# The last chunk of a layer-norm pipeline moved to other PSUM banks, and eight small turns of a QR step done another way

## The chip, the cores and the metric

One core of one Trainium2 chip runs the whole kernel in one launch. The metric is device time in microseconds (us). The engines are named as in the profile: PE is TensorE (PEld its weight loads), DVE is VectorE, ACT is ScalarE, POOL is GpSimd, SP is SyncE, which here only issues DMAs. Each engine runs its own list of instructions in order and waits on counting semaphores. PSUM has eight banks of 2 KB per partition; PE writes them, DVE and ACT read them.

## The reference

```python
h = _L0_tok_ref(x, w, b)            # softmax over windows of 8 samples, weighted sum: 128 x 94 tokens of 64
h = h + _L0_attn_ref(_layernorm(h), ...)
h = h + _L0_ffn_ref(_layernorm(h), ...)

# inside the attention, per batch row and head:
qkv = (x @ w_qkv.T + b_qkv)
qgr, _ = jnp.linalg.qr(q)
kgr, _ = jnp.linalg.qr(k)
attn_grass = jnp.einsum('bhnd,bhmd->bhnm', qgr, kgr) ** 2 * grassman_scale
dots = jnp.einsum('bhnd,bhmd->bhnm', q, k)
a = jnp.concatenate([dots * scale, dots ** 2 * riem_scale, attn_grass], axis=1)
a = softmax(conv_w @ batchnorm(a) + conv_b);  out = a @ v
```

Q of the QR step is not formed. The kernel takes the Gram matrix of each head's 8 columns (q.T q and k.T k), eliminates it and fixes the signs, and from that makes one 8 x 8 matrix per head that stands between q and k.

## The kernel before, in words

The program is a row of blocks. At the end of a block all engines meet (a barrier), and only then does the next one begin. Four matter here.

**Constants**, up to 26.9 us. **Tokens** (`pool_project`), from there to 228.3 us: the 64 pairs of batch rows come in, are scored and softmaxed. A loop of `STEPS` = 32 steps spreads the weights over the partitions by PE into `ps_spread` (four banks), DVE and POOL multiply and sum. Behind it runs a chain for each of `NCH` = 16 chunks of four pairs (`CP`), one chunk every two steps:

- `pads(c)` on DVE completes the tokens of the chunk, `centre(c)` on PE subtracts the mean (into `ps_c`), `squares(c)` on ACT writes the squares `sq` and a copy `xc`;
- `variance(c)` on PE, `deviation(c)` on ACT and `inverse(c)` on DVE give one over the deviation;
- `rows(c, h)` on PE multiplies by the weights of q, k and v, for halves h = 0 and 1, both into the two banks of `ps_tok`; `rows_out(c, h)` on DVE scales them into `tok` and raises `drained[h]`;
- `store(c)` on SP writes `tok` to DRAM by three DMAs; `grams(c)` on PE multiplies `tok` with itself into `ps_c`, `grams_out(c)` on ACT copies that to `own`, and `gram_sum(c)` on POOL sums it into `gram`.

Since both halves of `rows` use `ps_tok`, `rows(c, 1)` waits for `rows_out(c, 0)`. Since `ps_c` holds the centred tokens and the Gram matrices alike, `centre(c)` waits for `grams_out(c - 1)`. After step 31 nothing is left of the loop but the end of chunk 14 and all of chunk 15. SP waits for all stores before it meets the others.

**QR** (`orthogonalise`), 228.3 to 287.1 us. PE turns `gram` (eight 128 x 128 pieces, into `ps_turn`), DVE copies them to `aug` after it and POOL have filled the rest of `aug`, and then works down one long list: elimination, roots, signs, back-substitution, up to `m_sum`. PE turns `m_sum` in eight pieces of 128 x 128, and DVE copies them back to `m_t` in four copies. Beside this list, ACT copies `top` (a DMA of the first eight rows of each head) into `aug`; PE turns q and k of chunks 0 to 7 (`queries_keys`, 32 turns of 96 x 64 in a chunk, each two chunks ahead of ACT's copies at most); then PE and ACT prepare ten banks of expert weights (`EXPERT_BANKS`). ACT takes the roots ahead of the copy of bank number `ROOTS_AT` = 7, counted from 0. After the banks, q and k of chunks 8 to 15 follow.

**Attention** (`attend`), the rest: PE, DVE, ACT and POOL in a loop over 64 pairs, then projection and FFN. Its first instruction of weight is POOL's `m_blk<-m_t`.

Of the kernel before, what the change touches and what calls it, by code (L numbers as in the profile page):

```python
# [287 lines left out]
def pool_project(nc, x, x_g, x_in, ps_score, tokens, gram, v_dram, qk_dram, top_dram, qk_rows, rows_in, k):  # L288
# [4 lines left out]
    with ExitStack() as ctx:  # L293
# [34 lines left out]
        def halves(view):  # L328
            return view.rearrange("p (a t) -> p a t", a=2)

        def chunk_at(i, begun):

            c, odd = divmod(i - begun, 2)
            return c if not odd and 0 <= c < NCH else None

        @block.sync
# [33 lines left out]
        def _(pe):  # L370
# [21 lines left out]
            def centre(c):  # L392
                pe.wait_ge(s["ready"], c + 1)
                if c:
                    pe.wait_ge(s["std_done"], c)
                    pe.wait_ge(s["gram_out"], c)
                pe.matmul(ps_c[:, 0:W], k["cent_w"][:], tokens[:, span(c, CP), :].rearrange("p r m -> p (r m)"),
                          start=True, stop=True).then_inc(s["cent_done"], 1)

            def variance(c):  # L400
                pe.wait_ge(s["kept"], c + 1)
                for r in range(CP):
                    mm = pe.matmul(ps_c[0:NP, W + 2 * r:W + 2 * r + 2], sq[:, r, :], k["mean_w"][:, 0:128:64], start=True, stop=True)
                mm.then_inc(s["var_done"], 1)

            def rows(c, h):
                if h:
                    pe.wait_ge(drained[0], c + 1)
                elif c:
                    pe.wait_ge(drained[1], c)  # L410
                for e in range(2):
                    for b in range(2):
                        own_rows = slice(64 * b, 64 * b + 64)
                        mm = pe.matmul(ps_tok[:, b, 192 * e:192 * e + 192], xc[own_rows, 2 * h + e, :],
                                       k["w_tok"][own_rows, b, :], start=True, stop=True)
# [15 lines left out]
            for i in range(STEPS + 4):  # L431
                if i < STEPS:
                    spread(i // HP, 2 * (i % HP))
                c = chunk_at(i, 4)
                if c is not None:
# [5 lines left out]
                if i < STEPS:  # L441
                    spread(i // HP, 2 * (i % HP) + 1)
                c = chunk_at(i, 4)
                if c is not None:
                    rows(c, 1)
                c = chunk_at(i, 3)
                if c is not None:
                    centre(c)

        def parted(eng, g, part):  # L450
# [18 lines left out]
        def _(act):  # L469
# [24 lines left out]
            def squares(c):  # L494
                act.wait_ge(s["cent_done"], c + 1)
                if c:
                    act.wait_ge(s["var_done"], c)
                    act.wait_ge(s["tok_done"], 2 * c)
                act.activation(sq[:].rearrange("p r m -> p (r m)"), ps_c[:, 0:W], ACT.Square)
                act.activation(xc[:].rearrange("p r m -> p (r m)"), ps_c[:, 0:W], ACT.Copy).then_inc(s["kept"], 1)  # L500

            def deviation(c):
                act.wait_ge(s["var_done"], c + 1)
                if c:
                    act.wait_ge(s["rstd_done"], c)
                act.activation(std[:], ps_c[0:NP, W:W + 2 * CP], ACT.Sqrt, bias=k["ln_eps"][0:NP, 0:1]).then_inc(s["std_done"], 1)

# [8 lines left out]
            for i in range(STEPS + 4):  # L516
                c = chunk_at(i, 5)
                if c is not None:
                    grams_out(c)
                c = chunk_at(i, 4)  # L520
# [4 lines left out]
                c = chunk_at(i, 3)  # L525
# [33 lines left out]
        def _(dve):  # L559
# [39 lines left out]
            def rows_out(c, h):  # L599
# [6 lines left out]
                for e in range(2):  # L606
                    for b in range(2):
                        r = 2 * h + e
                        out = dve.scalar_tensor_tensor(out=tok[:, a, r, b, :], in0=ps_tok[:, b, 192 * e:192 * e + 192],
                                                       scalar=rstd[:, a, 2 * r + b:2 * r + b + 1], in1=k["bias_row"][:, 0, :],  # L610
# [56 lines left out]
def orthogonalise(nc, p, gram, m_t, top_dram, qk_dram, qk_rows, rows_in, q_cm, k_cm, k):  # L667
# [10 lines left out]
    with ExitStack() as ctx:  # L678
# [30 lines left out]
        marks = {}  # L709

        @block.sync
        def _(sp):
# [16 lines left out]
        def _(act):  # L729
# [812 lines left out]
```

## Time and profile before

| | us |
|---|---|
| median of 3 runs | 875.92 |
| lowest, highest | 872.6, 876.63 |
| the profiled execution | 875.29 |
| its span, first to last instruction | 873.4 |
| mean granted TensorE clock, as a share | 0.941 |

The profiled execution is 1.89 us longer than its span. Times in the rows below are from the span's start.

### The profile page before, as it was taken

The page shows a single profiled execution, that of the slowest core. Times are in us where ns is not written, and L with a number is a line of the kernel's source. Part 1 is how long each engine was busy: PE and PEld are TensorE (multiplying, and loading weights), DVE is VectorE, ACT ScalarE, POOL GpSimd, SP SyncE. Part 2 cuts the span into 40 slices and gives each one's busy share as a digit, 9 for nine tenths or more (in the row PEclk, how much of TensorE's full clock was granted, in tenths as well). Part 3 has the DMA queues.
Part 4 walks back from the last instruction along what each step waited for, and adds up shares of the span by engine and source line. Part 5 has one row for each costly group of instructions (what it writes and reads, how often), then busy time and mean ns, then how long its engine had stood idle before and what let it go on. Part 6 is the DMA issues. An engine that isn't in the chain of part 4 may idle for free.

```text
span 873.4 us, 39834 instructions
## 1 busy us (share of the span) xinstructions
PE 765.1 (88%) x16837; PEld 566.1 (65%) x16837; DVE 709.7 (81%) x1376; ACT 452.7 (52%) x943; POOL 515.0 (59%) x580
## 2 busy tenths in 40 slices
PE   3478898776695799999999999999999999799994
PEld 2245454444575577777777787777777877466663
DVE  4387878775598499999999999999999999767762
ACT  2362434322344365555565566655656556477773
POOL 3244444443000688888888888888888887222220
PEclk9798879878698699999999999999999999999998
DMA  8756662662580222222222222222222221011111
GB/s 291 294 170 199 201 193 65 131 129 59 156 146 2 63 65 67 65 71 67 73 64 65 65 64 64 64 66 66 73 73 65 64 64 45 1 24 30 28 29 33
DMA packets 89198, 77.63 MB, mean 89 GB/s; under 512 B 37145, under 2 KB 79708, under 8 KB 89052
## 3 DMA queue, kind: packets, MB, share of 16 engines
q1 hardware_dynamic: 88524, 73.83, 29.4%
q8 instruction: 131, 2.15, 1.0%
q10 hardware_dynamic: 528, 1.54, 0.5%
q14 instruction: 15, 0.12, 0.0%
HBM read 59.23 MB, written 13.04 MB: 83 GB/s over the span
## 4 chain that ended last, share of the span: by engine, by line
PE 50%; DVE 11%; issue 3%; ACT 1%; POOL 0%; POOLq 0%; ACTq 0%; DVEq 0%
PE ps_dot L1091 10%; PE ps_m L1115 8%; PE ps_a L1141 7%; PE ps_a L1133 7%; PE ps_a L1227 4%; DVE row_max_o L1351 3%; DVE row_max_e L1353 3%; PE ps_a L1104 3%; DVE row_max L1339 2%; DVE sums L1371 2%; PE ps_m L1077 2%; PE ps_a L1212 2%; PE ps_dot L1184 1%; PE ps_a L1235 1%; PE ps_m L1121 1%
## 5 line engine op out<-in xcount | busy, mean ns | idle before, releaser
L1270 ACT ACTIVATE sq<-ps_dot 128x376 f32<-128x376 f32 x384 | 165.2, 482 | 152.3 <-PE ps_dot L1091 144.3
L1091 PE MATMUL ps_dot<-q_st,k_blk 64*64 64x94 f32 x6144 | 170.5, 249 | 1.1 <-ACT sq L1270 0.8
L1091 PEld LDWEIGHTS ps_dot<-q_st,k_blk 64*64 64x64 f32 x6144 | 134.6, 134 | 53.0 <-issue 28.9
L1028 POOL TENSOR_TENSOR half<-prob 128x564 f32<-128x564 f32 x64 | 75.6, 1182 | 61.3 <-ACT prob L1265 61.3
L1013 POOL TENSOR_TENSOR v_blk<-v_rep,vmask 128x384 f32<-128x384 f32 x128 | 106.8, 856 | 7.1 <-PE ps_m L1121 5.2
L549 POOL TENSOR_TENSOR x_g<-x_g,w_odd 128x752 f32<-128x752 f32 x32 | 57.0, 1780 | 89.4 <-ACT w_odd L492 89.4
L1035 POOL TENSOR_TENSOR k_blk<-k_cm,hmask 128x768 f32<-128x768 f32 x64 | 96.8, 1513 | 1.8 <-PE ps_a L1133 1.8
L1037 POOL TENSOR_TENSOR k_mix<-k_cm,cols 128x768 f32<-128x768 f32 x64 | 96.9, 1514 | 0.0
L1339 DVE TENSOR_REDUCE row_max<-ps_a 128x94 f32<-128x564 f32 x128 | 89.4, 740 | 5.9 <-PE ps_a L1141 5.7
L1141 PE MATMUL ps_a<-sq,mix_w 64*32 64x282 f32 x2048 | 82.4, 406 | 0.3 <-ACT sq L1270 0.3
L1115 PE MATMUL ps_m<-prob,v_blk 128*64 128x94 f32 x1536 | 76.6, 248 | 1.1 <-ACT prob L1265 1.1
L1262 ACT ACTIVATE prob<-prob,head_const 128x564 f32<-128x564 f32 x64 | 49.1, 767 | 51.6 <-DVE prob L1361 51.6
L1133 PE MATMUL ps_a<-q_st,k_mix 64*64 64x94 f32 x3072 | 75.4, 243 | 0.5 <-DVE prob L1361 0.3
L1064 POOL COPY w_sel<-ffn_w 128x258 f32 x64 | 25.9, 404 | 77.9 <-DVE qk_rows L1427 52.3
L1115 PEld LDWEIGHTS ps_m<-prob,v_blk 128*64 128x64 f32 x1536 | 64.8, 136 | 8.7 <-ACT prob L1265 1.7
L385 PE MATMUL ps_spread<-parts,pair_sel 128*128 128x376 bf16 x256 | 60.4, 365 | 10.0 <-POOL parts L466 10.0
L1133 PEld LDWEIGHTS ps_a<-q_st,k_mix 64*64 64x64 f32 x3072 | 68.0, 134 | 1.1 <-issue 1.0
L1346 DVE TENSOR_TENSOR k_blk<-ps_m,hmask 128x768 f32<-128x768 f32 x64 | 61.3, 957 | 7.5 <-PE ps_dot L1091 4.9
L1371 DVE TENSOR_REDUCE sums<-half 128x94 f32<-128x282 f32 x128 | 60.0, 470 | 1.7 <-POOL half L1028 1.7
L1021 POOL TENSOR_TENSOR m_blk<-m_t,mask 128x128 f32<-128x128 f32 x64 | 26.0, 407 | 57.2 <-POOLq L678 57.2
L584 DVE TENSOR_REDUCE tokens<-x_g 128x94 f32<-128x752 f32 x64 | 57.9, 924 | 0.5 <-POOL x_g L549 0.5
L1141 PEld LDWEIGHTS ps_a<-sq,mix_w 64*32 64x32 f32 x2048 | 47.6, 106 | 9.1 <-ACT sq L1270 0.7
(221 smaller groups left out, 1440.2 us busy)
## 6 DMA issues: line engine op xcount, KB each, us to landing
v_rep<-v_rows SPq DMA_DIRECT2D x128, 192.0 KB, 3.1
x_g<-in_x_dram SPq DMA_DIRECT2D x15, 1500.0 KB, 7.8
qk_rows_kept<-tok SPq DMA_DIRECT2D x16, 384.0 KB
qk_rows<-qk_rows_kept SPq DMA_DIRECT2D x4, 1536.0 KB, 11.2
v_rows<-tok SPq DMA_DIRECT2D x16, 192.0 KB
q_st<-q_cm SPq DMA_DIRECT2D x64, 47.0 KB, 1.9
out_dram<-rows SPq DMA_DIRECT2D x16, 188.0 KB
x_g<-in_x_dram ACTq DMA_DIRECT2D x1, 1500.0 KB, 7.3
```

Of the source, the lines that this page charges most:

```text
L1013: vb = pool.tensor_tensor(v_blk[:, a, b].rearrange("p t (o d) -> p (t o) d", o=H), v_rep[:, a, b].rearrange("p (t o d) -> p (t o) d", o=H, ...
L1028: pool.tensor_tensor(half[:], prob[:, a, :, 0:3, :], prob[:, a, :, 3:6, :], ALU.add).then_inc(s["half_done"], 1)
L1035: pool.tensor_tensor(k_blk[:, a, :, 0], k_cm[:, span(i, 1), :].rearrange("p i (u m) -> p (i u) m", m=4).unsqueeze(2).broadcast_to([128, NT ...
L1037: pool.tensor_tensor(k_mix[:, a].rearrange("p t x o -> p (t x) o"), k_cm[:, span(i, 1), :].rearrange("p i m -> p (i m)").unsqueeze(2).broa ...
L1091: mm = pe.matmul(ps_dot[64 * v:64 * v + 64, (2 * g + b) % 3, N * c:N * c + N], k_blk[rows, a, SLOTS * (3 * v + g) + c].rearrange("p k h m ...
L1115: pe.matmul(ps_m[64 * b:64 * b + 64, AV_AT:AV_AT + N], v_blk[:, a, b, t, :], prob[:, a, b, t, :], start=(t == 0), stop=(t == NT - 1), skip ...
L1133: mm = pe.matmul(ps_a[half_of, BANK[b][t // 3], N * (t % 3):N * (t % 3) + N], k_mix[64 * b:64 * b + 64, a, t, 8 * w:8 * w + 8].rearrange(" ...
L1141: mm = pe.matmul(ps_a[32 * c:32 * c + 32, BANK[b][v], 0:3 * N], k["mix_w"][64 * v:64 * v + 64, :], sq[64 * v:64 * v + 64, b, c].rearrange( ...
L1270: act.activation(sq[:, b, :, g, :], ps_dot[:, (2 * g + b) % 3, 0:SLOTS * N].rearrange("p (c n) -> p c n", c=SLOTS), ACT.Square).then_inc(s ...
L1339: dve.tensor_reduce(top[:, b, :], bass.AP(ps_a[:].tensor, 1024 * b, [[4 * 512, 128], [1, N], [512, 2], [N, 3]]), AX.XY, ALU.max).then_inc( ...
L1346: dve.tensor_tensor(k_blk[:, a, :, 1], ps_m[:, KT_AT:KT_AT + NP].rearrange("p (u m) -> p u m", m=4).unsqueeze(2).broadcast_to([128, NT * S ...
L1371: dve.tensor_reduce(sums[:, b], half[:, b].rearrange("p t n -> p n t"), AX.X, ALU.add).then_inc(s["sums_done"], 1)
```

## The change

It has three parts. First, the last chunk (c = `LAST` = 15) has other PSUM banks: its centred tokens and its variance go to bank 0 of `ps_spread`, and its rows of h = 0 to banks 1 and 2 of it; its rows of h = 1 stay in `ps_tok`. `centre(15)` then waits only for the tokens. PE's list has chunk 15 up to its rows in step 32, ahead of the Gram matrices of chunk 14, and these of chunk 15 wait for `grams_out(14)`. ACT's list has `squares(15)` and `deviation(15)` in step 32 too, ahead of `grams_out(14)`. Second, the eight turns of `gram` are `transpose` where they were `matmul` with the identity. Third, of the four copies of turned sums into `m_t`, ACT takes the two of partitions 64 to 127.

```diff
+        def centred(c):
+            return ps_spread[:, 0, :] if c == LAST else ps_c[:]
+
+        def rows_bank(c, h, b):
+            return ps_spread[0:NP, 1 + b, :] if c == LAST and h == 0 else ps_tok[:, b, :]
...
             def centre(c):
                 pe.wait_ge(s["ready"], c + 1)
-                if c:
+                if 0 < c < LAST:
                     pe.wait_ge(s["std_done"], c)
                     pe.wait_ge(s["gram_out"], c)
...
             def rows(c, h):
-                if h:
+                if h and c < LAST:
                     pe.wait_ge(drained[0], c + 1)
-                elif c:
+                elif c and (h or c < LAST):
                     pe.wait_ge(drained[1], c)
...
                 pe.wait_ge(s["std_done"], c + 1)
+                if c == LAST:
+                    pe.wait_ge(s["gram_out"], c)
...
+                if i == STEPS:
+                    centre(LAST)
+                    variance(LAST)
+                    for h in range(2):
+                        rows(LAST, h)
...
+                if i == STEPS:
+                    squares(LAST)
+                    deviation(LAST)
...
+        def turned_back(b, n):
+
+            q = slice(64 * b, 64 * b + 64)
+            return (m_t[q, :, 4 * n:4 * n + 4].rearrange("p i d -> p d i"),
+                    ps_turn[q, 2 + n, :].rearrange("p (d i b) -> p d i b", d=4, b=2)[:, :, :, b])
...
+            for n in range(2):
+                act.wait_ge(m_turned, n + 1)
+                act.activation(*turned_back(1, n), ACT.Copy)
...
-                for b in range(2):
-                    q = slice(64 * b, 64 * b + 64)
-                    step(dve.tensor_copy(m_t[q, :, 4 * n:4 * n + 4].rearrange("p i d -> p d i"),
-                                         ps_turn[q, 2 + n, :].rearrange("p (d i b) -> p d i b", d=4, b=2)[:, :, :, b]))
+                step(dve.tensor_copy(*turned_back(0, n)))
...
-                mm = pe.matmul(ps_turn[:, e // 4, 128 * (e % 4):128 * (e % 4) + 128], gram[:, :, e], k["ident"][:], start=True, stop=True)
+                mm = pe.transpose(ps_turn[:, e // 4, 128 * (e % 4):128 * (e % 4) + 128], gram[:, :, e], k["ident"][:])
```

What stands on PE at the end of the token block, before. L385 is `spread`, L397 `centre`, L403 `variance`, L414 `rows`, L426 `grams`; after the last spread come four rows of chunk 14 and four of chunk 15.

```order
L385 MATMUL ps_spread<-parts,pair_sel 128x376 x4
L397 MATMUL ps_c<-tokens,cent_w 128x384
L403 MATMUL ps_c<-mean_w,j_sq 96x2 x4
L414 MATMUL ps_tok<-w_tok,j_xc 96x192 x8
L426 MATMUL ps_c<-tok 32x32 x32
L397 MATMUL ps_c<-tokens,cent_w 128x384
L403 MATMUL ps_c<-mean_w,j_sq 96x2 x4
L414 MATMUL ps_tok<-w_tok,j_xc 96x192 x8
L426 MATMUL ps_c<-tok 32x32 x32
```

The same place of PE with the change (the lines of the five helpers are now 398, 410, 416, 427 and 441).

```order
L398 MATMUL ps_spread<-parts,pair_sel 128x376 x4
L410 MATMUL ps_c<-tokens,cent_w 128x384
L416 MATMUL ps_c<-mean_w,j_sq 96x2 x4
L427 MATMUL ps_tok<-w_tok,j_xc 96x192 x8
L410 MATMUL ps_spread<-tokens,cent_w 128x384
L416 MATMUL ps_spread<-mean_w,j_sq 96x2 x4
L427 MATMUL ps_spread<-w_tok,j_xc 96x192 x4
L427 MATMUL ps_tok<-w_tok,j_xc 96x192 x4
L441 MATMUL ps_c<-tok 32x32 x64
```

The whole chain of chunk 15 up to its rows moved ahead of the Gram matrices of chunk 14, which now stand in one row with those of chunk 15.

What stands on DVE at the end of the QR block, before (L773 is the helper of the list, L833 doubles `m_sum`, L839 copies back, L678 is the block's end).

```order
L773 TENSOR_TENSOR prods<-wq,aug 128x8
L773 TENSOR_TENSOR m_sum<-m_sum,prods 128x8
L833 COPY m_sum<-m_sum 128x8x64
L839 COPY m_t<-ps_turn 64x4x64 x4
L678 UNCONDITIONAL_BRANCH
```

And with the change.

```order
L805 TENSOR_TENSOR prods<-wq,aug 128x8
L805 TENSOR_TENSOR m_sum<-m_sum,prods 128x8
L865 COPY m_sum<-m_sum 128x8x64
L869 COPY m_t<-ps_turn 64x4x64 x2
L701 UNCONDITIONAL_BRANCH
```

Two of the four copies left DVE; they stand at the end of ACT's list, behind its last copy of k.

## Rows read from the trace of the kernel before

**Rows 1.** The head of the page: the span.

```profile
span 873.4 us, 39834 instructions
```

**Rows 2.** Timeline, chunks 14 and 15: start, duration, instruction, [idle before <-releaser].

```profile
209.68 0.16 DVE L590 TENSOR_REDUCE tokens<-tokens 128x8 f32<-128x8 f32 x1
...
211.38 1.08 PE L426 MATMUL ps_c<-tok 94*32 94x32 f32 x64 [1.64 <-issue]
...
212.52 0.38 ACT L512 ACTIVATE own<-ps_c 128x256 f32<-128x256 f32 x1 [5.78 <-PE ps_c L426]
...
213.05 1.62 PE L397 MATMUL ps_c<-tokens,cent_w 128*128 128x384 f32 x2 [0.58 <-ACT own L512]
...
217.00 1.60 PE L414 MATMUL ps_tok<-w_tok,j_xc 64*96 64x192 f32 x8
...
218.75 1.39 DVE L609 SCALAR_TENSOR_TENSOR tok<-ps_tok,j_rstd,bias_row 96x192 f32<-96x192 f32 x4 [1.14 <-PE ps_tok L414]
...
220.19 1.60 PE L414 MATMUL ps_tok<-w_tok,j_xc 64*96 64x192 f32 x8 [1.59 <-DVE tok L609]
221.93 1.39 DVE L609 SCALAR_TENSOR_TENSOR tok<-ps_tok,j_rstd,bias_row 96x192 f32<-96x192 f32 x4 [1.80 <-PE ps_tok L414]
...
224.32 0.55 SPq L351 DMA_DIRECT2D top_rows<-tok  x1
...
226.25 0.32 POOL L540 TENSOR_TENSOR gram<-own 128x64 f32<-128x64 f32 x1
```

**Rows 3.** SP's waits over the whole run: one of them.

```profile
SPq L367 <- DMA top_rows<-tok: 2.9, 1, 2.9
```

**Rows 4.** Timeline, chunk 14 at the higher clock.

```profile
203.77 0.87 PE L397 MATMUL ps_c<-tokens,cent_w 128*128 128x384 f32 x2
...
206.37 0.89 PE L414 MATMUL ps_tok<-w_tok,j_xc 64*96 64x192 f32 x8
```

**Rows 5.** Windows: stretch, length, busy time (instructions) by engine, PEclk, DMA share, GB/s.

```profile
207.00:210.40 3.40, 1.16 (x12) 0.57 (x8) 2.90 (x8) 0.00 (x0) 0.96 (x3) 0.99 0.00 0
210.50:228.20 17.70, 8.35 (x154) 5.75 (x154) 3.76 (x12) 1.90 (x5) 2.77 (x6) 0.50 0.32 71
```

**Rows 6.** Timeline, the start of the QR block.

```profile
228.33 4.16 PE L845 MATMUL ps_turn<-ident,gram 128*128 128x128 f32 x16 [3.83 <-PEq L293]
...
229.55 0.44 POOL L726 MEMSET aug<- 128x16 f32 x8 [2.98 <-DVE aug L775]
...
232.60 1.43 DVE L779 COPY aug<-ps_turn 128x512 f32<-128x512 f32 x1 [0.47 <-PE ps_turn L845]
232.99 2.04 ACT L741 ACTIVATE aug<-top 128x1024 f32<-128x1024 f32 x1 [8.05 <-DMA top<-top_rows]
...
235.76 1.09 DVE L790 TENSOR_TENSOR prods_t<-fac,aug 128x896 f32<-128x896 f32 x1
```

**Rows 7.** Timeline around the roots.

```profile
255.34 0.32 DVE L797 COPY diag<-aug 128x128 f32<-128x128 f32 x1
...
256.10 0.60 ACT L753 ACTIVATE ffn_w<-ps_turn 128x512 f32<-128x512 f32 x1 [1.16 <-PE ps_turn L877]
...
257.00 0.95 DVE L800 RECIPROCAL rs<-rs 128x128 f32<-128x128 f32 x1 [1.34 <-ACT rs L751]
```

**Rows 8.** Timeline of PE alone: q and k of chunks 2 to 7.

```profile
236.82 8.14 PE L856 MATMUL ps_turn<-ident,qk_rows 96*64 96x96 f32 x192 [0.67 <-ACT k_cm L738]
```

**Rows 9.** Timeline, the end of the QR block.

```profile
282.86 1.97 PE L885 MATMUL ps_turn<-ident,m_sum 128*128 128x128 f32 x8 [10.06 <-DVE m_sum L833]
284.08 2.56 DVE L839 COPY m_t<-ps_turn 64x256 f32<-64x256 f32 x4 [1.28 <-PE ps_turn L885]
...
287.18 0.41 POOL L1021 TENSOR_TENSOR m_blk<-m_t,mask 128x128 f32<-128x128 f32 x1 [57.19 <-POOLq L678]
```

**Rows 10.** Windows, columns as in rows 5.

```profile
232.60:234.20 1.60, 1.60 (x22) 1.60 (x24) 1.56 (x2) 1.21 (x1) 0.00 (x0) 0.50 1.00 316
...
104.60:118.20 13.60, 13.03 (x108) 7.41 (x109) 11.39 (x21) 6.25 (x11) 6.78 (x7) 0.50 0.59 194
```

More of the change, by code:

```diff
@@ L329, in halves @@
             return view.rearrange("p (a t) -> p a t", a=2)
+        LAST = NCH - 1
+        def centred(c):
+            return ps_spread[:, 0, :] if c == LAST else ps_c[:]
+        def rows_bank(c, h, b):
+            return ps_spread[0:NP, 1 + b, :] if c == LAST and h == 0 else ps_tok[:, b, :]
         def chunk_at(i, begun):
@@ L334, in chunk_at, with early_chunk_at @@
             return c if not odd and 0 <= c < NCH else None
+        def early_chunk_at(i, begun):
+            c = chunk_at(i, begun)
+            return c if c != LAST else None
         @block.sync
@@ L393, in centre @@
                 pe.wait_ge(s["ready"], c + 1)
-                if c:
+                if 0 < c < LAST:
                     pe.wait_ge(s["std_done"], c)
                     pe.wait_ge(s["gram_out"], c)
-                pe.matmul(ps_c[:, 0:W], k["cent_w"][:], tokens[:, span(c, CP), :].rearrange("p r m -> p (r m)"),
+                pe.matmul(centred(c)[:, 0:W], k["cent_w"][:], tokens[:, span(c, CP), :].rearrange("p r m -> p (r m)"),
                           start=True, stop=True).then_inc(s["cent_done"], 1)
@@ L402, in variance @@
                 for r in range(CP):
-                    mm = pe.matmul(ps_c[0:NP, W + 2 * r:W + 2 * r + 2], sq[:, r, :], k["mean_w"][:, 0:128:64], start=True, stop=True)
+                    mm = pe.matmul(centred(c)[0:NP, W + 2 * r:W + 2 * r + 2], sq[:, r, :], k["mean_w"][:, 0:128:64], start=True, stop=True)
                 mm.then_inc(s["var_done"], 1)
             def rows(c, h):
-                if h:
+                if h and c < LAST:
                     pe.wait_ge(drained[0], c + 1)
-                elif c:
+                elif c and (h or c < LAST):
                     pe.wait_ge(drained[1], c)
@@ L433, in _ @@
                     spread(i // HP, 2 * (i % HP))
-                c = chunk_at(i, 4)
+                c = early_chunk_at(i, 4)
                 if c is not None:
@@ L442, in _ @@
                     spread(i // HP, 2 * (i % HP) + 1)
-                c = chunk_at(i, 4)
+                c = early_chunk_at(i, 4)
                 if c is not None:
                     rows(c, 1)
-                c = chunk_at(i, 3)
+                c = early_chunk_at(i, 3)
                 if c is not None:
                     centre(c)
+                if i == STEPS:
[3 more added lines that the diff above has]
+                        rows(LAST, h)
         def parted(eng, g, part):
@@ L498, in squares @@
                     act.wait_ge(s["tok_done"], 2 * c)
-                act.activation(sq[:].rearrange("p r m -> p (r m)"), ps_c[:, 0:W], ACT.Square)
-                act.activation(xc[:].rearrange("p r m -> p (r m)"), ps_c[:, 0:W], ACT.Copy).then_inc(s["kept"], 1)
+                act.activation(sq[:].rearrange("p r m -> p (r m)"), centred(c)[:, 0:W], ACT.Square)
+                act.activation(xc[:].rearrange("p r m -> p (r m)"), centred(c)[:, 0:W], ACT.Copy).then_inc(s["kept"], 1)
             def deviation(c):
@@ L505, in deviation @@
                     act.wait_ge(s["rstd_done"], c)
-                act.activation(std[:], ps_c[0:NP, W:W + 2 * CP], ACT.Sqrt, bias=k["ln_eps"][0:NP, 0:1]).then_inc(s["std_done"], 1)
+                act.activation(std[:], centred(c)[0:NP, W:W + 2 * CP], ACT.Sqrt, bias=k["ln_eps"][0:NP, 0:1]).then_inc(s["std_done"], 1)
             def grams_out(c):
@@ L519, in _ @@
                     grams_out(c)
-                c = chunk_at(i, 4)
+                c = early_chunk_at(i, 4)
                 if c is not None:
@@ L524, in _ @@
                     odd_weights(i)
-                c = chunk_at(i, 3)
+                c = early_chunk_at(i, 3)
                 if c is not None:
                     squares(c)
+                if i == STEPS:
+                    squares(LAST)
+                    deviation(LAST)
                 if i < STEPS - HP:
```

4 lines of the change are left out of this document (2 added, 2 removed).

## The prediction

> **What bounds the kernel now.** The span is 873.4 us [rows 1] and the profiled execution 875.29, so 1.89 us lie outside it; the median is 875.92, 0.63 above that execution. I read the timeline first, because the three edits sit at the ends of blocks, where all engines meet and nothing of the next block can cover a delay. Three places matter.
>
> The end of the token block is one thread. The tokens of chunk 15 are complete at 209.84, but `centre(15)` starts at 213.05: it waits for ACT's `own` copy (212.52 to 212.90) of chunk 14's Gram matrices (211.38) [rows 2]. From there the thread runs centre, squares, variance, rows (217.00), `rows_out` (218.75), rows again (220.19, 1.59 us idle for DVE), `rows_out` again (221.93 to 223.32). SP issues the last of three stores at 224.32 to 224.87 and waits 2.9 us for its landing [rows 3], to about 227.8; POOL is done at 226.57. The next block's PE starts at 228.33 [rows 6]. So SP's stores end the block, POOL is 1.2 us earlier.
>
> The QR block is DVE's list, with one gate: its reciprocal at 257.00 idled 1.34 us for ACT's roots, though `diag` was ready at 255.66 [rows 7]. ACT could not take the roots sooner: they stand behind its copy of an expert bank (256.10), which had waited for PE. Going back along that queue: PE works on the experts when q and k of chunks 2 to 7 are turned, and it starts these at 236.82, after 0.67 us of idle for ACT's first copies [rows 8]; ACT is late because it waited 8.05 us for the DMA of `top`, to 232.99, and then copied 2.04 us [rows 6]. So from the block's start to the roots the time is set by this DMA, ACT and PE, and DVE has slack: about 0.9 us, if the roots (0.3 us and two hand-overs) were taken at once.
>
> The end of the block is PE's turns of `m_sum` (282.86 to 284.83), DVE's four copies (284.08 to 286.64) and the barrier; POOL starts the next block at 287.18 [rows 9].
>
> **The change, part 1: chunk 15.** `centre(15)` can start when `tokens` is ready and PE has done chunk 14's rows (209.75): at about 209.92 instead of 213.05, which is 3.13 sooner. What stands behind it on PE is the 64 Gram products of chunk 14; for them waits only ACT's `own` and POOL, costed below. Up to 210.4 the clock is at its higher level and then at the lower [rows 5]. At the lower one centre takes 1.62 and ends 1.66 before ACT starts; at the higher 0.87 [rows 2, 4]. The new one runs 0.5 us at the higher, which is 57% of it, and the other 43% cost 0.70: ACT starts 1.21 after its start instead of 1.66, 0.45 sooner. The rest up to the first `rows_out` is unchanged: 217.00 falls to 213.42, 218.75 to 215.17. The second half no longer waits for DVE: eight passes follow on PE, each 0.16 (192 columns at 1.2 GHz, and 8 x 0.16 + 0.32 is the 1.60 of the row), so they are done at 213.42 + 2.56 + 0.32 = 216.30, and DVE, busy with the first half until 216.56, goes on without a break: to about 217.93 instead of 223.32. That is 5.4 us.
>
> Does it reach the block's end? SP's path moves whole: 5.4. POOL's: chunk 14's Gram matrices now run at 216.4 to 217.5, `own` to 217.95, POOL's three sums (1.55 us) to 219.55; chunk 15's products 218.0 to 219.1, `own` must wait for those sums, 219.6 to 220.0, and POOL ends at 221.6. SP ends at 227.8 - 5.4 = 222.4, still last, with 0.8 to spare. The stores of chunk 14 have left 6 us before. The bounds of this part: if the clock is at the lower level from the start, 4.95; if it stays at the higher to the end, centre to rows takes 2.60 instead of 3.95, rows 0.89 and 0.77 more for the second half, DVE ends at 209.92 + 2.60 + 0.89 + 0.15 + 2.78 = 216.4, which is 6.9. Ahead of the fall PE was busy 1.16 of 3.40 us [rows 5]; the new centre adds about 0.5 us, still half or less, so I take 5.4.
>
> **Part 2: the turns of `gram`.** Eight matmuls in 16 passes take 4.16 us; eight transposes of that very shape, at the same clock, are 8 instructions in 1.97 [rows 6, 9]. DVE's second copy into `aug` starts at 232.60 for want of them. The first could start when POOL has filled `aug`, 229.99, so the copies would end near 232.85 instead of 234.03: 1.2 sooner. But `prods_t` reads ACT's copy of `top`, ready at 235.03, so it can start only 0.7 sooner than 235.76 [rows 6]. And all of that flows into the wait for the roots, which stand at the same distance from the block's start as before: the slack there grows from 0.9 to 1.6. This part is worth 0; the cover is the gate at 257.00, and without it the part would be worth 0.7.
>
> **Part 3: the copies back.** Four DVE copies take 2.56, so 0.64 each. With two on DVE the second starts when the last turn lands, 284.83, and ends at 285.5. ACT's pair runs beside it. The trace has no such ACT copy: one of 256 elements from PSUM took 0.38 [rows 2], the strided 1,024 of `top` 2.04 [rows 6], so 0.38 to 0.6; with the first of them a little late, ACT ends by 285.3 to 285.7. Gain 0.9 to 1.1, I take 1.0; if ACT and DVE took turns on the bank it would be 0.
>
> **The sum.** 875.29 - 5.4 - 0 - 1.0 = 868.9 for an execution like the profiled one; beside the median, 875.92 - 6.4 = **869.5**.
>
> **The rivals.**
> *A, the clock in q and k is lost.* Before, PE had no gap from 228.33 until 236.2, and the clock rose at 234.3 in it; then 192 passes took 8.14 us, 42 ns each. At the lower level 22 take 1.60, 73 ns [rows 8, 10]. Now PE has 2.2 us less to do and must still wait for ACT until 8.5 us after the block's start. At the lower clock its work ends 5.7 to 7.2 us into it, sooner if the clock rises in between: a gap of up to 3 us like the one ahead of the fall at 210.4 [rows 5]. If q and k then meet the lower clock, each microsecond costs 0.42 on the path to the roots, and nothing covers it, since ACT's queue is what DVE waits for. A low stretch of 3.5 to 7 us costs 1.5 to 2.9: 871.0 to 872.4. For it: the gap. Against: it must fall badly against the clock's own changes, about half the cases. The Trainium skill ("TensorE: Matmul & The Clock Gate", Part 4) says that the higher clock does not engage for transposes, which do not count as busy in the same way; by that rule the 2 us of transposes add to the gap and the clock rises later too. No row of this trace shows it either way: its only transposes of that size stand alone at the lower clock.
> *B, the clock holds through chunk 15.* PE's work is closer together at the fall. Part 1 gives 6.9: 868.0.
> *C, the block's end is held by something else.* If the landing of the last store or the barrier does not follow DVE whole, for instance because POOL or the two chunks' stores come into each other's way, 2 to 3 us of part 1 are lost: 871.5 to 872.5. Against: 0.8 us of room at POOL, 6 us between the stores.
> *D, slower.* The same gap as in A, but the low clock stays through q and k and into the experts: 192 x 31 ns = 5.9, and from there on every microsecond of PE's expert work at half speed costs about half of one. The gain of 6.4 is gone when the low stretch outlasts q and k by 1 us, some 15 us in all. A stretch of 13.6 us at the lower clock with PE busy 13.03 of it exists [rows 10], so it can happen; but at this place PE's passes follow without gaps, as they did at 234.3 when the clock rose. About 878 if the experts are in it.
>
> **How the numbers follow.** The forecast 0.50 (own range 868 to 871), A 0.28, B 0.11, C 0.07, D 0.04. 0.5% is 4.4 us, about what a measurement of this kernel tells from no change: faster is below 871.5, slower above 880.3. Nearly all of the forecast and B, and some 0.35 of A, are faster: 0.49 + 0.11 + 0.09 = 0.69; of D a half is slower: 0.02; the remaining 0.29 is the same. The range 867 to 873 takes in B and A.
>
> **What would show it.** DVE's last `rows_out` should end near 218 and PE's first transpose start near 223; PE should go from rows to rows of chunk 15 without idle. The eight turns should be 8 instructions in 2 us, DVE's wait for the roots longer (about 2 us), and the distance from the block's start to the reciprocal unchanged at 28.7; if it has grown, it is A, and PEclk over q and k of chunks 2 to 7 shows it. The block should end 1.0 us sooner after the turns of `m_sum`. The prediction is wrong if SP or POOL holds the token block beyond 224, or if that distance grows by over 2.

## The result, and the profile after

The changed kernel took 866.25 us, median of four runs (864.78 to 867.52), against 876.06 for four runs of the kernel before. The ratio is 0.9896, 95% interval 0.9861 to 0.993, so the gain is 9.1 us by the ratio and lies between 6.1 and 12.2. Faster, as forecast. The forecast was 869.5, in a range of 867 to 873, so the median is 0.75 below the lower end of the range.

The head of the page of the changed kernel, and its table of engines.

```profile
span 865.7 us, 39818 instructions
...
PE 764.4 (88%) x16829; PEld 564.6 (65%) x16829; DVE 708.4 (82%) x1374; ACT 454.2 (52%) x945; POOL 514.6 (59%) x580
```

The profiled execution took 867.52, the longest of the four. The timeline of the end of the token block and the start of the QR block (start, duration, instruction, [idle before <-releaser]):

```profile
208.01 0.16 DVE L613 TENSOR_REDUCE tokens<-tokens 128x8 f32<-128x8 f32 x1
208.23 0.91 PE L410 MATMUL ps_spread<-tokens,cent_w 128*128 128x384 f32 x2
...
210.87 1.05 PE L427 MATMUL ps_spread<-w_tok,j_xc 64*96 64x192 f32 x8
211.72 1.49 PE L427 MATMUL ps_tok<-w_tok,j_xc 64*96 64x192 f32 x8
212.07 1.39 DVE L632 SCALAR_TENSOR_TENSOR tok<-ps_spread,j_rstd,bias_row 96x192 f32<-96x192 f32 x4 [0.59 <-PE ps_spread L427]
213.38 1.38 DVE L632 SCALAR_TENSOR_TENSOR tok<-ps_tok,j_rstd,bias_row 96x192 f32<-96x192 f32 x4
...
216.14 0.48 SPq L364 DMA_DIRECT2D top_rows<-tok  x1
...
218.06 0.32 POOL L563 TENSOR_TENSOR gram<-own 128x64 f32<-128x64 f32 x1
...
219.82 1.94 PE L874 MATMUL ps_turn<-ident,gram 128*128 128x128 f32 x8 [3.88 <-PEq L293]
...
221.51 2.90 DVE L811 COPY aug<-ps_turn 128x512 f32<-128x512 f32 x2 [0.53 <-POOL aug L755]
...
223.16 2.04 ACT L770 ACTIVATE aug<-top 128x1024 f32<-128x1024 f32 x1 [6.40 <-DMA top<-top_rows]
```

Against [rows 2]: centre now follows the tokens at once, PE goes from rows to rows without idle, and DVE's second group, at 213.38, follows its first without a gap. Against [rows 6]: the turns of `gram` are 8 instructions in 1.94 and DVE's two copies run together. And one line that I had not foreseen: ACT starts the copy of `top` 3.34 after the block's start (223.16 - 219.82); before it was 4.66.

Around the roots, and at the end of the QR block:

```profile
245.72 0.32 DVE L829 COPY diag<-aug 128x128 f32<-128x128 f32 x1
...
249.14 0.30 ACT L780 ACTIVATE rs<-diag 128x128 f32<-128x128 f32 x1
...
249.54 0.95 DVE L832 RECIPROCAL rs<-rs 128x128 f32<-128x128 f32 x1 [3.50 <-ACT rs L780]
...
275.42 1.97 PE L914 MATMUL ps_turn<-ident,m_sum 128*128 128x128 f32 x8 [10.08 <-DVE m_sum L865]
...
276.57 0.63 ACT L788 ACTIVATE m_t<-ps_turn 64x256 f32<-64x256 f32 x1 [10.37 <-PE ps_turn L914]
...
277.50 0.61 DVE L869 COPY m_t<-ps_turn 64x256 f32<-64x256 f32 x1 [0.24 <-PE ps_turn L914]
...
278.64 0.77 POOL L1050 TENSOR_TENSOR m_blk<-m_t,mask 128x128 f32<-128x128 f32 x2 [57.16 <-POOLq L701]
```

DVE's wait for the roots is 3.50 now; it was 1.34 [rows 7]. And the windows of the changed kernel (stretch, length, busy time by engine, PEclk, DMA share, GB/s): chunk 15 up to the clock's fall, the stretch behind it, then q and k of chunks 0 to 7 before and after the clock's rise.

```profile
208.20:211.70 3.50, 2.51 (x18) 1.87 (x20) 1.59 (x5) 1.14 (x3) 0.00 (x0) 0.97 0.32 61
211.80:218.40 6.60, 3.50 (x138) 2.71 (x134) 2.69 (x8) 0.77 (x2) 2.77 (x6) 0.50 0.64 148
222.20:232.20 10.00, 10.00 (x130) 9.80 (x128) 9.79 (x13) 6.63 (x12) 0.00 (x0) 0.51 0.84 233
232.30:238.00 5.70, 5.23 (x128) 5.04 (x123) 5.56 (x11) 5.13 (x9) 0.00 (x0) 1.00 0.84 167
```

Put together, the distances between the same events of the two profiles (starts from the rows; "tokens" is the end of the last TENSOR_REDUCE):

| from, to | before | after | difference |
|---|---|---|---|
| span's start, tokens | 209.84 | 208.17 | -1.67 |
| tokens, QR's first turn | 18.49 | 11.65 | -6.84 |
| QR's first turn, reciprocal | 28.67 | 29.72 | +1.05 |
| reciprocal, first turn of `m_sum` | 25.86 | 25.88 | +0.02 |
| that turn, `m_blk` | 4.32 | 3.22 | -1.10 |
| `m_blk`, end of the span | 586.2 | 587.1 | +0.8 |

These sum to the 7.7 between the spans. The first and the last line hold nothing that the change touches; in the profiles of all kernels of this study the tokens end anywhere from 203.8 to 210.2. So two of the three parts are seen at once (-6.84, -1.10), and the QR block is both better than forecast (`top`) and worse (the clock). The experiments take that apart.

### The profile page after: what moved, and what is told of

Same layout as the page of the kernel before. It is cut to its first block, busy times and chain, and to the rows that moved or that the text cites. A ratio compares the mean times of both kernels' runs of the same rounds, so it can differ in the third digit from the quotient of the medians.

```text
span 865.7 us, 39818 instructions
## 1 busy us (share of the span) xinstructions
PE 764.4 (88%) x16829; PEld 564.6 (65%) x16829; DVE 708.4 (82%) x1374; ACT 454.2 (52%) x945; POOL 514.6 (59%) x580
## 4 chain that ended last, share of the span: by engine, by line
PE 52%; DVE 10%; issue 3%; ACT 1%; POOL 0%; POOLq 0%; ACTq 0%; DVEq 0%
PE ps_dot L1120 10%; PE ps_m L1144 8%; PE ps_a L1170 8%; PE ps_a L1162 7%; PE ps_a L1256 4%; DVE row_max_o L1380 3%; DVE row_max_e L1382 3%; PE ps_a L1133 3%; DVE row_max L1368 2%; PE ps_m L1106 2%; PE ps_a L1241 2%; DVE sums L1400 2%; PE ps_dot L1213 1%; PE ps_a L1264 1%; PE ps_m L1150 1%
## 5 line engine op out<-in xcount | busy, mean ns | idle before, releaser
L1170 PEld LDWEIGHTS ps_a<-sq,mix_w 64*32 64x32 f32 x2048 | 46.6, 106 | 10.9 <-issue 1.2
```

Of the source, the lines that this page charges most:

```text
L1170: mm = pe.matmul(ps_a[32 * c:32 * c + 32, BANK[b][v], 0:3 * N], k["mix_w"][64 * v:64 * v + 64, :], sq[64 * v:64 * v + 64, b, c].rearrange( ...
```

## The experiments

Single executions of one and the same kernel scatter here: the kernel before gave 870.49 to 879.34 in 30 executions beside the first set. Even a median of some ten executions tells only about 2.5 us. A difference smaller than that is not read from the times here. So for each kernel I also read these distances in its profile, worked out from the timeline as above, in us: **A**, from the tokens to the end of DVE's last `rows_out`; **B**, from QR's first turn to ACT's copy of `top`; **C**, to the first turn of chunk 2 of q and k; **D**, to `diag` ready; **E**, to the reciprocal; **F**, from the first turn of `m_sum` to `m_blk`; and "rise", the time from QR's first turn to the rise of TensorE's clock from its lower level (PEclk 0.50) to its higher one (1.00).

| | parts | A | B | C | D | E | F | rise |
|---|---|---|---|---|---|---|---|---|
| before | none | 13.48 | 4.66 | 8.49 | 27.32 | 28.66 | 4.31 | 5.9 |
| after | all | 6.58 | 3.34 | 7.19 | 26.22 | 29.72 | 3.22 | 12.1 |
| e1 | all | 8.95 | 3.40 | 7.25 | 26.23 | 27.41 | 3.22 | 4.1 |
| e14 | all | 8.05 | 3.42 | 7.27 | 26.22 | 27.44 | 3.21 | 4.5 |
| e2 | 1 | 8.95 | 3.31 | 7.22 | 27.32 | 27.77 | 4.31 | 5.0 |
| e3 | 2 | 13.48 | 4.24 | 8.06 | 26.23 | 28.23 | 4.31 | 6.3 |
| e4 | 3 | 13.55 | 5.31 | 9.16 | 27.34 | 29.32 | 3.22 | 5.0 |
| e5 | 1, 3 | 6.56 | 3.49 | 7.37 | 27.32 | 27.77 | 3.22 | 5.4 |
| e7 | all, roots early | 8.47 | 3.44 | 7.29 | 26.20 | 26.65 | 3.21 | 3.3 |
| e8 | 1, 3, roots early | 8.96 | 3.32 | 7.21 | 27.31 | 27.75 | 3.21 | 5.0 |
| e9 | all, one bank pair | 9.94 | 3.37 | 7.21 | 26.21 | 27.38 | 3.21 | 6.0 |
| e11 | none, code shifted | 14.18 | 4.60 | 8.44 | 27.33 | 28.61 | 4.31 | 5.7 |
| e12 | all, code shifted | 8.95 | 4.79 | 8.62 | 26.75 | 31.98 | 3.22 | 15.3 |
| e13 | all, old order | 9.90 | 4.39 | 8.22 | 26.35 | 30.03 | 3.22 | see there |

### The change again, and each part alone

The changed kernel again: nine executions, one of them profiled (e1), and later one more profiled execution (e14).

> The changed kernel once more, in more rounds. Two theories of the 3.3 us by which it beat the forecast. Theory 1, the clock held through chunk 15: part 1 is worth 6.9 instead of 5.4 and the rest is what runs differ by; then the difference to the kernel before is 7.5 to 9 us. Theory 2, the four runs happened to fall low: the difference comes to 6 to 7 us. In the profile, from the end of DVE's last token pad to the first PE instruction of the QR block: 11.6 us by theory 1, 13.1 by theory 2 (18.5 before).

Part 1 alone: parts 2 and 3 are undone.

```diff
-                mm = pe.transpose(ps_turn[:, e // 4, 128 * (e % 4):128 * (e % 4) + 128], gram[:, :, e], k["ident"][:])
+                mm = pe.matmul(ps_turn[:, e // 4, 128 * (e % 4):128 * (e % 4) + 128], gram[:, :, e], k["ident"][:], start=True, stop=True)
...
-            for n in range(2):
-                act.wait_ge(m_turned, n + 1)
-                act.activation(*turned_back(1, n), ACT.Copy)
```

> Part 1 alone (chunk 15's banks and order), the turns of gram and the copies back as before. If part 1 is all but 1 us of the gain: 6 to 8 us faster than before. If the forecast's 5.4 was right and something else gave the rest: 5 to 6. From the block's start to the roots' reciprocal 28.7 us, as before, if only transposes lengthen it (29.7 with the change).

Part 2 alone: the kernel before with the one line `pe.transpose`.

> Part 2 alone (the turns of gram by transposes). The theory that the roots' gate hides it: 0, with DVE's wait for the roots at about 2 us instead of 1.3. The rival, that transposes cost the clock in q and k of chunks 2 to 7: 1 to 3 us slower than before, PE at the lower clock until 10 us or more after the block's start (6.0 before), and the roots later by as much.

Part 3 alone: the kernel before with the two copies on ACT.

> Part 3 alone (two of the four copies back on ACT): 1.0 to 1.1 us faster, and 3.2 us from the first turn of m_sum to POOL's first instruction of the attention instead of 4.3. The rival is that it is too small to be seen in the times; the profile decides.

Parts 1 and 3: the changed kernel with `pe.matmul` for the turns of `gram`.

> Parts 1 and 3, the turns of gram left as matmuls. Theory 1, part 2 is hidden and harmless: the time of the whole change within 1 us, DVE's reciprocal of the roots 27.8 us after the block's start (with DVE's own list as the bound, diag ready at 27.3). Theory 2, the transposes cost the clock in q and k: the clock rises 4 to 7 us after the block's start here, and this kernel is 1 to 2 us faster than the whole change.

Measured, beside the kernel before on the same chip (874.44 us for e1 to e4, 873.84 for e5), with the gain by the ratio:

| | us | ratio, interval | gain |
|---|---|---|---|
| e1, all | 865.86 | 0.991 [0.9881, 0.994] | 7.9 (5.2 to 10.4) |
| e2, part 1 | 866.25 | 0.9924 [0.9892, 0.9956] | 6.6 (3.8 to 9.4) |
| e3, part 2 | 873.78 | 0.9998 [0.9971, 1.0025] | 0.2 (-2.2 to 2.5) |
| e4, part 3 | 872.03 | 0.9967 [0.9939, 0.9994] | 2.9 (0.5 to 5.3) |
| e5, parts 1 and 3 | 866.82 | 0.9916 [0.9886, 0.9945] | 7.3 (4.8 to 10.0) |

Part 1 carries nearly all of it and part 2 alone is worth nothing that can be told. Of e1's two theories neither holds whole: the gain, 7.9, lies in the range of the first, but the distance from the tokens to QR's first turn is 13.96 and not its 11.6, so a held clock does not explain it. e14 took 867.99 in its one execution, and the late rise of the clock did not come again in e1 or e14. The table of distances gives the sizes. A falls from 13.48 and 13.55 to 8.95, 8.05 or 6.56. The later the clock falls to its lower level, the shorter A is: 1.4 us or more ahead of the end of the tokens in e1 and e2, 0.5 behind it in e14, 3.3 behind it in after and e5. F falls by 1.1 wherever part 3 is in and nowhere else. And E is not the forecast's constant: 28.66 before, 27.77 with part 1 alone, 27.41 and 27.44 with all three, where the clock rose early. It goes with B: E - C is 20.17 in before and e3 and 20.16 in e4 and e1, so the roots stand at a fixed distance behind PE's start on chunk 2, and that stands 3.8 to 3.9 behind ACT's copy of `top`. With part 1 alone (e2) E - C is 20.55, since there `diag` is the later one (D + 0.45 = E). The profile of e1 shows the block as I had forecast it, with the roots earlier:

```profile
226.41 8.14 PE L885 MATMUL ps_turn<-ident,qk_rows 96*64 96x96 f32 x192 [1.44 <-ACT k_cm L767]
...
246.18 0.30 ACT L780 ACTIVATE rs<-diag 128x128 f32<-128x128 f32 x1
...
246.58 0.95 DVE L832 RECIPROCAL rs<-rs 128x128 f32<-128x128 f32 x1 [1.19 <-ACT rs L780]
```

The 192 passes take 8.14, as before [rows 8]; QR's first turn stood at 219.16 here.

### Is the gate at the roots what hides part 2?

ACT takes the roots two expert banks sooner, with transposes (e7) and with matmuls (e8).

```diff
-ROOTS_AT = 7
+ROOTS_AT = 5
```

> The whole change, and ACT takes the roots ahead of expert bank 5 instead of 7. If ACT's queue is the gate: the reciprocal starts at 26.7 us after the block's start, 0.4 to 0.5 after diag, whatever the clock in q and k does (27.4 and 29.7 in two profiles of the change), and the kernel gains 0.7 to 3 us, so 9 to 11 faster than before. If the gate is a story, nothing changes.

> The same with the turns of gram as matmuls. Without the gate part 2 should be seen: the reciprocal 1.1 us later than with the transposes (diag was ready at 27.3 against 26.2), so at 27.8. If transposes are worth nothing even then, the two kernels agree within 0.3 us there.

e7 took 866.33 (ratio to before 0.9906 [0.9875, 0.9938]), e8 865.64 (0.9901 [0.987, 0.9932]); neither can be told from the change by its time. The 9 to 11 us expected of e7 are not seen in it either: the ratio gives 8.2 (5.4 to 10.9). The distances tell: in e7 DVE waits 0.44 for the roots instead of 1.19.

```profile
247.55 0.32 DVE L829 COPY diag<-aug 128x128 f32<-128x128 f32 x1
247.90 0.31 ACT L780 ACTIVATE rs<-diag 128x128 f32<-128x128 f32 x1 [2.57 <-DVE diag L829]
...
248.31 0.95 DVE L832 RECIPROCAL rs<-rs 128x128 f32<-128x128 f32 x1 [0.44 <-ACT rs L780]
```

Without the gate the transposes are worth 27.75 - 26.65 = 1.1, with it and part 1 they are worth 27.77 - 27.41 = 0.36. With it and without part 1 (e3) E is 0.43 below that of before, and B is 0.42 below: E follows the landing of `top`, and nothing is left over for the transposes. The gate is shown. My price without it, 0.7, was low: with `top` landing sooner, its copy no longer holds `prods_t` back, and the full 1.1 to 1.2 of the second copy into `aug` shows. It was right for the landing I had assumed: where that copy came late in kernels with transposes, `diag` was ready 21.96 behind it (e12: 26.75 - 4.79, e13: 26.35 - 4.39), so at the 4.66 of before it would be ready at 26.62, which is 0.7 ahead of 27.32.

### What in part 1 is the banks, what the order?

One pair of banks for the rows of chunk 15, so the second half waits for DVE again; the rest of part 1 stays.

```diff
-            return ps_spread[0:NP, 1 + b, :] if c == LAST and h == 0 else ps_tok[:, b, :]
+            return ps_tok[:, b, :]
...
-                if h and c < LAST:
+                if h:
                     pe.wait_ge(drained[0], c + 1)
-                elif c and (h or c < LAST):
+                elif c:
                     pe.wait_ge(drained[1], c)
```

> The whole change, but both halves of chunk 15's rows in ps_tok, so that the second waits for DVE as before. Splits part 1: from the end of the last pads to the end of DVE's last rows_out 8.5 us (higher clock) or 10.9 (lower) instead of 6.6 or 9.0, 13.5 before. So the early centre alone keeps 2.6 to 5 us, and this kernel is 1 to 2 us slower than the whole change. Rival: the second bank pair is worth nothing, and the distance stays at 6.6 to 9.0.

868.97 us, 0.9936 [0.9911, 0.9961]. PE's idle time of before is back, row for row as in [rows 2]:

```profile
216.53 1.60 PE L427 MATMUL ps_tok<-w_tok,j_xc 64*96 64x192 f32 x8 [1.59 <-DVE tok L632]
```

A is 9.94 here and 8.05 in e14, where the clock fell at nearly the same place: the second pair of banks is worth 1.9, and 13.48 - 9.94 = 3.5 is the earlier start.

Then the other half: the banks of the change, but chunk 15 at its old place in PE's list, behind the Gram matrices of chunk 14.

```diff
-                if i == STEPS:
+                if i == STEPS + 1:
                     centre(LAST)
```

> The whole change, but PE takes chunk 15 behind the Gram products of chunk 14, as before; the other banks are kept. If it is the order on PE that gives the early centre: it starts at 2.7 us after the last pads, not at 0.1 us, and the distance from the pads to DVE's last rows_out is 9.2 to 11.5 us (6.6 to 9.0 with the change, 13.5 before), 2.6 us slower than the change. If the wait for ACT's copy was all, the order costs nothing.

872.51 us, 0.998 [0.9957, 1.0004]: most of the gain is gone. In its profile the clock held 3.3 us past the tokens, as it did in after, and A was 9.90 against 6.58: PE's order is worth 3.3, since these Gram products wait until DVE has scaled the rows of chunk 14. The time is some 6 us worse than e1's by the ratios, though; in the profile the other 2.6 lie in E. In this run the clock fell again in q and k, as rival A had it. Windows of e13:

```profile
223.30:228.60 5.30, 5.30 (x60) 4.97 (x60) 4.63 (x6) 1.33 (x1) 0.44 (x8) 0.53 0.84 239
228.70:231.00 2.30, 0.62 (x16) 0.43 (x12) 2.28 (x3) 2.30 (x8) 0.00 (x0) 1.00 1.07 293
231.00:240.00 9.00, 8.90 (x176) 8.93 (x178) 8.86 (x14) 6.71 (x12) 0.00 (x0) 0.81 0.68 168
```

The clock rose 5.4 after QR's first turn, PE stood idle for ACT's first copies (busy 0.62 of 2.30), the clock fell 8.85 after that turn, 0.6 after the first turn of chunk 2 of q and k, and rose again at 12.3. E was 30.03 instead of 27.4. The gap was there (1.78 ahead of chunk 2), but it is not the whole cause: PE stood idle as long at the same place in e4 (1.78) and longer in e7, and there the clock held and the 192 passes took 8.14. The row of e7:

```profile
228.96 8.14 PE L885 MATMUL ps_turn<-ident,qk_rows 96*64 96x96 f32 x192 [1.88 <-ACT k_cm L767]
```

### Why does `top` land sooner?

In the DMA records of before, e3, e4 and e13 a packet of 16,384 bytes of the instruction queue, so code for an engine, starts 0.92 to 1.05 after QR's first turn, among the 128 packets of 4 KB of `top`, and takes 1.07 to 1.9 us. In the kernels that have part 1 whole, or all of it but the second bank pair (e9), the packet starts 2.4 to 2.8 after that turn and takes 0.9 to 1.0. e13 has the banks of part 1 but not its order on PE, so it is the order that goes with the late packet. The DMA view of before, over the time in which `top` is on its way (queue: packets, MB, share of 16 engines; below, median us to landing):

```profile
q1 hardware_dynamic: 105, 0.43, 53.7%
q8 instruction: 1, 0.02, 3.2%
...
top<-top_rows SPq DMA_DIRECT2D x1, 512.0 KB, 4.7
```

And of the changed kernel:

```profile
q1 hardware_dynamic: 119, 0.46, 58.6%
...
top<-top_rows SPq DMA_DIRECT2D x1, 512.0 KB, 3.4
```

The theory: that packet delays the packets of `top` queued behind it on its DMA engine. The rival: `top_rows` is read sooner or more easily because its stores ended at another time. First I tried to move the packet by shifting PE's code, with small matmuls in the block of constants (8 in before, e11; 3 in the change, e12).

```diff
+            pe.wait_ge(pool_step, marks["score_w"])
+            for _ in range(8):
+                pe.matmul(ps_t[:, 1, 300:301], k["ident"][:], k["ident"][:, 0:1], start=True, stop=True)
```

> The kernel before, with eight one-column matmuls on PE ahead of its first turns, where PE waits 9 us for the parameters: they cost nothing there and shift all that follows in PE's code by 32 instructions. In three profiles without part 1 a 16 KB packet of the instruction queue starts 1.0 us after the QR block's start, among the packets of top, and ACT's copy of top starts at 4.2 to 5.3; in six with part 1 it starts at 2.4 or later and the copy at 3.3 to 3.5. Theory 1, the code load delays top: shifted, the packet falls ahead of the block and the copy starts at 3.3. Theory 2, part 1 brings top sooner in another way (stores further behind): the copy stays at 4.2 or later.

> The whole change with three such matmuls, which shift PE's code by 12 instructions, so that the packet should start 1 us after the block's start. Theory 1: the copy of top falls back to 4.2 to 5.3 and the roots to 28.2 or more (27.4 without). Theory 2: it stays at 3.3 to 3.5.

e11 took 875.89 (1.0014 [0.9987, 1.0041]), e12 870.75 (0.9966 [0.9941, 0.9992]). The packet did not go where I meant it to: it started at 2.28 in e11 and 2.45 in e12. In both the last two packets of `top` start only when it has ended or about then (3.17 and 3.60 in e11, 3.34 and 3.77 in e12; the packet ended at 3.18 and 3.35), and ACT's copy starts at 4.60 and 4.79. That fits the theory, but e12's packet lies where that of e2 (2.41) and e8 (2.46) does and did harm there, so its time alone doesn't settle it. I take it that it must also fall on a DMA engine that still has packets of `top` to move; the records at hand do not name the engine of a packet, so this is not shown.

So I kept PE from fetching: it waits until `top` is in, ahead of the turns of `gram`, in before (e15) and in the change (e18).

```diff
+            pe.wait_ge(top_in, 16)
             for e in range(D):
```

> The kernel before, with PE held at the QR block's start until top has landed, so that PE's next code load comes after top. If the code load among the packets of top is what delays it: ACT's copy of top starts 3.3 to 3.5 us after the block's start (4.66 before, 4.2 to 5.3 in other kernels where a load met it). If the kernel without part 1 gets top late for another reason: 4.2 or more. The time as a whole says nothing here, since PE starts 3 us later.

> The same hold in the changed kernel, as its control: ACT's copy of top at 3.3 to 3.5 us as without the hold (3.34 to 3.42 in four profiles) by both theories.

One execution each: 880.04 beside 876.71 for before, and 870.2; single times like these say nothing. With PE held, its first turn no longer marks the block's start, so I take SP's issue of `top`, which stands 0.05 ahead of that turn in before and after. In e15 this issue comes 4.98 behind DVE's last `rows_out` (4.96 in before) and 3.97 behind the issue of the last store (3.96), so the stores and the end of the token block are those of before; and no packet of code comes until 7.05 after the block's start. Its timeline and its DMA view:

```profile
226.41 0.35 SPq L713 DMA_DIRECT2D top<-top_rows  x1
...
229.88 1.99 ACT L741 ACTIVATE aug<-top 128x1024 f32<-128x1024 f32 x1 [6.82 <-DMA top<-top_rows]
```

```profile
q1 hardware_dynamic: 317, 0.65, 68.8%
...
top<-top_rows SPq DMA_DIRECT2D x1, 512.0 KB, 3.4
```

`top` lands after 3.4 instead of 4.7, and ACT's copy stands at 3.42, the value of the kernels with part 1; the rival through the stores is out, since they are those of before. In e18 the copy stands at 3.22 and the packet at 6.7. So holding PE moved the packet in both kernels, which makes it PE's code, and without it `top` is as early in the kernel before as in the change. That rests on one profile, but none of the other profiles without the order of part 1 has the copy before 4.24. What decides when the packet is fetched stays open. PE's place in its code alone does not: after and e13 have the same number of instructions on PE, run as many of them ahead of the block, and have the packet at 2.56 and 0.92.

### Do transposes keep the clock down?

Rival A stood on two legs: a gap, and what the Trainium skill ("TensorE: Matmul & The Clock Gate", Part 4) says, that the higher clock does not engage for transposes. Two kernels stretch the turns of `gram`, so that they last through the moment of the rise: each turn five times as a transpose (e16), twice as a matmul (e17, with parts 1 and 3). The extra turns rewrite the same banks.

```diff
-            for e in range(D):
+            for e in range(5 * D):
+                last, e = e >= 4 * D, e % D
...
-                if e % 4 == 3:
+                if last and e % 4 == 3:
```

> The changed kernel with the eight transposes of gram issued five times over (40, some 8.5 us of nothing else on PE from the block's start; only the last eight raise the semaphore). If transposes do not count towards the clock, it is still at the lower level when they end; if they count like matmuls, it rises within 7 us of the block's start, as it did at 5.0 to 5.9 in six profiles with matmuls.

> The control: parts 1 and 3 with the eight matmuls of gram issued twice (7.7 us at the lower clock). Both theories: the clock rises within 7 us of the block's start, before they end.

867.55 and 869.46 us in one execution each. In e16 PE did nothing but transposes for 6.99, and the clock rose 4.9 after the first of them, no later than it does in e2, e5 and e8 with their matmuls. Its row and its windows:

```profile
217.85 6.99 PE L875 MATMUL ps_turn<-ident,gram 128*128 128x128 f32 x40 [4.23 <-PEq L293]
```

```profile
217.80:223.20 5.40, 5.34 (x27) 5.38 (x28) 0.91 (x1) 1.97 (x2) 0.44 (x8) 0.54 0.74 211
223.30:224.80 1.50, 1.50 (x16) 1.38 (x15) 0.30 (x1) 0.55 (x4) 0.00 (x0) 1.00 1.03 302
```

PEclk is 0.54 in the first stretch, the lower level, and 1.00 in the second, the higher one, and PE ran transposes in both. In the matmul kernel e17 the clock rose 4.9 after the first turn.

Of the other kernels one thing must be known for this question: only the turns of `gram` are transposes in them. q and k are turned by `matmul` with the identity in every kernel (16 turns of a chunk in 32 passes; not 32 turns, as I wrote of the kernel before). So with part 2 PE ran some 1.9 us of transposes and then matmuls.

## Why the prediction was right or wrong, point by point

**What bounds the kernel** was read rightly: the end of chunk 15 as one thread up to SP's stores, the roots' gate, ACT behind `top` in front of it. From the end of the last `rows_out` to QR's first turn it is 5.00 to 5.08 in every kernel of the table (5.01 before, 5.06 after), so the block's end follows DVE whole and POOL is never the last: rival C did not happen.

**Part 1** was right in mechanism and size. In e14, where the clock fell about where I had put it, A is 8.05 and the gain 13.48 - 8.05 = 5.4, the forecast's number. e7, with the low clock from 0.2 ahead of the tokens' end, lies at the lower bound (13.48 - 8.47 = 5.0; forecast 4.95). e1 and e2 lie 0.5 below it (4.5): the clock was low already in the rows of chunk 14, these held PE, and `centre(15)` started 0.5 later, which my bound left out. after and e5 are at the upper one (6.9; forecast 6.9, rival B; its terms add up to 7.0). In these the clock did fall before the last rows (PEclk 0.50 from 211.80) and it cost nothing, as DVE's passes of 1.39 were the bound by then. Over the profiles of the table A is 13.67 as the mean of four without the part and 8.2 of eight with all of it: 5.5.

**Part 2** was put at nothing, on the step "the roots, which stand at the same distance from the block's start as before". **This step failed.** The gate was there (e7, e8), but its own distance was no constant: it hangs on the landing of `top`, which I had taken for a fixed 4.7 us transfer. A packet of PE's code among its packets had made it 1.3 longer (e15, without that packet: 3.4), and with part 1 that packet comes later. Where the clock rose early, E fell to 27.77 with part 1 and to 27.41 with part 2 as well: 0.9 that belong to part 1 and 0.36 to part 2, and no term of the sum had either. The prediction asked for "unchanged at 28.7" and, if it had grown, for rival A; that it could shrink was not considered. "Slack grows to 1.6" was near: 27.41 - 0.45 - 26.23 = 0.7 of it was left after the roots had moved up by 1.25; with the roots at their old 28.66 it would be 2.0. With part 2 alone (e3) it is 28.23 - 0.45 - 26.23 = 1.55, and DVE's wait for the roots is the forecast's 2.0. Taken alone, then, part 2 was worth nothing, as forecast; what was missing is that part 1 moves the gate.

**Part 3**: forecast 1.0, measured 1.1 (4.31 to 3.22). ACT's strided copy takes 0.62 to 0.63, a little above my 0.38 to 0.6, and it runs beside DVE's 0.61 on the other partitions of the same bank without a delay.

**The sum** as measured is 5.5 + 0.9 + 0.36 + 1.1 = 7.9 instead of 6.4. That is the 7.9 of e1, and within the 6.1 to 12.2 of the first result. The failed step, 1.3 us, does not by itself bring the time below 867: 869.5 - 1.3 is 868.2. The rest is the base and scatter. The 875.92 that I subtracted from was the median of three executions, and 30 others of the same kernel, on the chip of e1, had 874.44, which is 1.5 lower; four executions on either side leave the remaining half microsecond, and 876.06 - 866.25 = 9.8 as a difference, to chance. Part 1 alone and all three parts cannot be told apart by their times.

**Rival A** came up, in the very execution that was profiled: in after PE was busy 10.00 of 10.00 us at 0.51, the rise came 12.1 after QR's first turn instead of 4 to 6, and E was 29.72 instead of 27.4. By E - C, 22.53 instead of 20.16, it cost 2.4, inside my 1.5 to 2.9. But it did not come by the way I had drawn: there was no gap, since PE was busy all the time, so that the price came out right is in part luck. It came again in e12 (rise at 15.3, E - C 23.36, so 3.2), where PE did stand idle for 1.36 ahead of chunk 2, and behind a gap of 1.78 in e13. Its row in e12, against the 8.14 of [rows 8]:

```profile
226.49 11.34 PE L887 MATMUL ps_turn<-ident,qk_rows 96*64 96x96 f32 x192 [1.36 <-ACT k_cm L769]
```

Of the profiles in the table it shows in 3 of 8 with transposes and in none of 6 with matmuls. Three that fell at random on the 14 would all have transposes with a chance of 56 in 364, 0.15, so these counts leave it open. The Trainium skill ("TensorE: Matmul & The Clock Gate", Part 4) would make transposes the reason, and the runs speak against it. In e16 the clock rose while PE ran transposes alone. In after PE ran matmuls without a break from 1.87 behind the block's start, and the rise came 10.2 after the first of these, when in the kernels whose turns are all matmuls it came 4.9 to 5.9 after the first; if the 1.9 us of transposes counted for nothing, that would put the rise some 7 to 8 us behind the block's start, by these rows, and not 12.1. And in e1, e7 and e14 the same transposes went with a rise at 3.3 to 4.5. A gap explains it no better: it was absent in after, and gaps of 1.78 and 1.88 in e4 and e7 did no harm. Why the clock rose late in after and e12 and fell again in e13 stays open. **Rival D** did not come: the longest low stretch ended in q and k.

## What to carry to other kernels

At a barrier, a thread of small dependent steps is worth its full length: giving the last round other buffers and an earlier place in each queue gained 3.5 by the start and 1.9 by the second pair of banks, and all of it reached the block's end. A wait that gates a stretch is no constant because the change doesn't touch it: follow it back to its own source, and if that is a DMA, list every packet on its way, code packets of the instruction queue among them. Where single executions scatter by more than the effect, compare distances between the same two events over several profiles, and look at the clock before giving a difference a cause.

## What the runs showed of the hardware

- A 16,384-byte packet of PE's code on the instruction queue took 0.9 to 1.9 us. Among the packets of a 512 KB transfer it moved its landing from 3.4 us (e15, PE held) to 4.7 (before), and ACT's use of it from 3.2 to 3.5 up to 4.2 to 5.3.
- PE's clock rose from its lower to its higher level while only f32 128 x 128 transposes ran (e16, 4.9 us after the first).
- One and the same kernel met the rise of the clock 4.1, 4.5 and 12.1 us after a block's start in three profiles (e1, e14, after), the last with PE busy for 10.00 of 10.00 us at 0.51; that late rise cost 2.4 us.
- PE idle for 1.78 us at the higher clock was followed by its fall in e13; idle for 1.78 and 1.88 at the same place it was not in e4 and e7.
- ACT and DVE read the two halves of the partitions of one PSUM bank at the same time, 0.63 and 0.61 us for 64 x 256, as fast as DVE alone (0.64).
